# Cross-attention in two-step cycles of five TensorE runs, with four probability buffers

## What is computed

```python
def _L0_xattn_ref(hidden_states, audio_tokens, attention_mask, Wq, bq, Wk, bk, Wv, bv, Wo, bo, ...):
    q = proj(hs, Wq, bq, S); k = proj(at, Wk, bk, T); v = proj(at, Wv, bv, T)     # 16 heads of 16
    scores = jnp.einsum('bhsd,bhtd->bhst', q, k) / scale
    ...                                                     # clip, mask to -10000, clip to -50..50
    probs = jax.nn.softmax(scores, axis=-1)
    ctx = jnp.einsum('bhst,bhtd->bhsd', probs, v)
    delta = rs * (ctx @ Wo.T + bo)                          # then layernorm, added to x

x = x + _L0_attn_ref(_layernorm(x), ...)
x = x + _L0_xattn_ref(_layernorm(x), ctx_2048, mask_BxS2_ik0, ...)
x = x + _L0_ffn_ref(_layernorm(x), ...)                     # bit_linear(silu(gate) * val)
```

## Times and profile before

| | us |
|---|---|
| median of 3 timed runs | 1391.47 (1391.31 to 1391.74) |
| the profiled execution, its own time | 1393.63 |
| its span, first to last instruction | 1391.8 |
| TensorE busy in the span | 1369.9 |
| VectorE / ScalarE / GpSimd busy | 996.4 / 719.7 / 512.0 |
| mean granted TensorE clock | 0.998 of full speed |

### The profile page before, as it was taken

The page is one execution under the profiler, slowest core; times in us unless marked ns, Lnnn a source line. Parts: engine busy times, 40 slices in busy tenths (PEclk is TensorE's granted clock), DMA queues, the critical chain, the costliest instruction groups (busy, mean ns, idle before and its releaser), DMA issues.

```text
span 1391.8 us, 55872 instructions
## 1 busy us (share of the span) xinstructions
PE 1369.9 (98%) x25409; PEld 1171.4 (84%) x25409; DVE 996.4 (72%) x1824; ACT 719.7 (52%) x943; POOL 512.0 (37%) x491
## 2 busy tenths in 40 slices
PE   8999999999999999999999999999999999999997
PEld 6788888886888888888888888888888888888884
DVE  5688788785346867777676867677776868677766
ACT  3545454543555555555555555555554555555550
POOL 2656666551324233333323332433333242333310
PEclk9999999999999999999999999999999999999999
DMA  7010001010411211121212121121212112111100
GB/s 193 1 36 1 32 1 32 2 52 1 127 55 47 65 47 50 47 65 32 68 32 78 51 62 50 47 65 32 65 32 80 42 55 65 48 51 47 51 3 8
DMA packets 38957, 66.81 MB, mean 48 GB/s; under 512 B 3749, under 2 KB 36962, under 8 KB 38722
## 3 DMA queue, kind: packets, MB, share of 16 engines
q1 hardware_dynamic: 38722, 63.24, 15.6%
HBM read 61.40 MB, written 1.84 MB: 45 GB/s over the span
## 4 chain that ended last, share of the span: by engine, by line
PE 72%; DVE 2%; issue 0%; POOL 0%; DVEq 0%
PE proj_ps L1479 20%; PE proj_ps L1470 20%; PE score_ps L1497 15%; PE sum_ps L1522 13%; PE side_ps L1557 2%; PE side_ps L1571 1%; PE side_ps L1539 1%; PE side_ps L1564 1%; DVE amax L1357 0%; DVE hidden L1379 0%; DVE sig L1389 0%; DVE hidden L1390 0%; PE side_ps L1546 0%; DVE exps L1279 0%; DVE totals L1301 0%
## 5 line engine op out<-in xcount | busy, mean ns | idle before, releaser
L1231 ACT ACTIVATE exps<-score_ps 125x1792 f32<-125x1792 f32 x192 | 320.4, 1669 | 431.0 <-PE score_ps L1497 431.0
L1279 DVE TENSOR_SCALAR exps<-exps,top 125x896 f32<-125x896 f32 x384 | 287.9, 791 | 21.8 <-ACT exps L1231 17.5
L1497 PE MATMUL score_ps<-spread,keys 32*125 32x112 f32 x6144 | 219.0, 279 | 0.0
L1270 DVE COPY vals<-proj_ps 125x512 f32<-125x512 f32 x192 | 129.5, 687 | 116.7 <-PE proj_ps L1479 114.4
L1522 PEld LDWEIGHTS sum_ps<-exps,vals 125*32 125x32 f32 x12288 | 163.1, 110 | 47.1 <-issue 34.2
L1497 PEld LDWEIGHTS score_ps<-spread,keys 32*125 32x125 f32 x6144 | 184.8, 183 | 15.4 <-issue 0.3
L1522 PE MATMUL sum_ps<-exps,vals 125*32 125x56 f32 x12288 | 191.6, 215 | 0.0
L1159 POOL TENSOR_TENSOR low<-raw_early,high 128x500 fp32r<-128x500 f32 x64 | 84.5, 1322 | 216.8 <-PE proj_ps L1470 215.9
L1159 POOL TENSOR_TENSOR low_early<-raw_early,high_early 128x500 fp32r<-128x500 f32 x62 | 89.4, 1459 | 168.7 <-PE proj_ps L1470 168.7
L1223 ACT ACTIVATE keys<-proj_ps,b_k 128x500 f32<-128x500 f32 x192 | 129.9, 677 | 23.9 <-PE proj_ps L1470 20.4
L331 POOL TENSOR_TENSOR swapped<-swapped,sin 128x448 f32<-128x448 f32 (+1 forms) x69 | 81.0, 1175 | 85.6 <-ACT swapped L615 80.3
(11 more groups left out here) (187 smaller groups left out, 2702.7 us busy)
## 6 DMA issues: line engine op xcount, KB each, us to landing
raw_early<-in_ctxT SPq DMA_DIRECT2D x64, 500.0 KB, 4.2
raw<-in_ctxT SPq DMA_DIRECT2D x32, 500.0 KB, 3.6
w_q<-in_attn_Wq SPq DMA_DIRECT2D x4, 512.0 KB, 9.6
out<-y_out SPq DMA_DIRECT2D x16, 112.0 KB, 2.5
rows<-in_x SPq DMA_DIRECT2D x1, 1344.0 KB, 18.1
raw_early<-in_attn_Wo SPq DMA_DIRECT2D x1, 1024.0 KB, 17.5
raw_early<-in_ffn_gate_wT SPq DMA_DIRECT2D x1, 1024.0 KB, 5.3
raw_early<-in_ffn_val_wT SPq DMA_DIRECT2D x1, 1024.0 KB, 4.9
```

The lines of the kernel that those rows point to most:

```text
L1231: nc.scalar.activation(exps[t % 2][:, :, :, :].rearrange("p h r n -> p r h n"), score_ps[0:TILE, :, 0:2 * QW].rearrange("p r (h n) -> p r ...
L1270: nc.vector.tensor_copy(vals[r][:, 2 * q:2 * q + 2, :, 0:HD], proj_ps[q][0:TILE, :].rearrange("p (k h d) -> p k h d", k=2, d=HD))\
L1279: nc.vector.tensor_scalar(tile, tile, LIMIT_LO, top[:, n, at:at + 1], ALU.max, ALU.min)\
L1497: ins = nc.tensor.matmul(score_ps[0:TILE, r, to:to + HE * S], keys[c % 2][32 * r:32 * r + 32, k, (at + half) * TILE:(at + half + 1) * TILE ...
```

## The change

It does four things in `block_b`.

1. The number of probability buffers `exps` goes from 2 to 4 (`SLOTS`), and the exponential of step `t` waits for the value product of step `t - 4` instead of `t - 2`.
2. TensorE goes over a chunk's two steps in one cycle: scores of the even step, pieces 0 and 1, scores of the odd step, the value products of both steps *of the cycle before*, pieces 2 and 3. The steps after attention keep their numbers: an even one comes behind the even scores, an odd one behind the value products.
3. ScalarE makes both exponentials of the cycle first, then the copies of the two keys pieces with the `split_high` between them.
4. VectorE clips the probabilities in their own step (no longer one late), and makes both values copies at the end of the cycle, behind the step after attention of the odd step. `read_sums` comes behind the clip of the even steps 0 and 6.

```diff
-GATES = (7, 8)
-AFTER = (2, 5)
+TWINS = NT // 2
+SLOTS = 4
...
-        exps = [sb(f"exps{n}", [TILE, 2, HR, QW]) for n in range(2)]
+        exps = [sb(f"exps{n}", [TILE, 2, HR, QW]) for n in range(SLOTS)]
...
-                    act.wait_ge(probs_used, NT * i + t - 1)
+                    act.wait_ge(probs_used, NT * i + t - SLOTS + 1)
...
# ScalarE
             def body(i, first, last):
-                for t in range(NT):
-                    c, half = divmod(t, 2)
-                    x = PC * i + c
-                    exp_twin(i, t, not first or t >= 2)
-                    if half == 0:
-                        for p in range(DC):
-                            if not (last and c == PC - 1):
-                                keys_out(x + 1, p, (c + 1) % 2)
-                            if not (last and c >= PC - 2):
-                                split_high((c + 2) % 3, 2 * i + (c + 2) // 3 + 1, c % 2, p)
-                    if not first and t in GATES:
-                        gate_tanh(i - 1, GATES.index(t))
+                for m in range(TWINS):
+                    x = PC * i + m
+                    exp_twin(i, 2 * m, not first or 2 * m >= SLOTS)
+                    if not first and m == 4:
+                        gate_tanh(i - 1, 1)
+                    exp_twin(i, 2 * m + 1, not first or 2 * m + 1 >= SLOTS)
+                    for p in range(DC):
+                        if not (last and m == PC - 1):
+                            keys_out(x + 1, p, (m + 1) % 2)
+                        if not (last and m >= PC - 2):
+                            split_high((m + 2) % 3, 2 * i + (m + 2) // 3 + 1, m % 2, p)
+                    if not first and m == 3:
+                        gate_tanh(i - 1, 0)
...
# VectorE
-                for t in range(NT):
-                    c, half = divmod(t, 2)
+                for m in range(TWINS):
+                    e, o = 2 * m, 2 * m + 1
+                    if e in AHEAD and e in tail:
+                        tail[e]()
                     for k in range(2):
-                        if t:
-                            limit(i, t - 1, k)
-                        elif not first:
-                            limit(i - 1, NT - 1, k)
-                    if t == 1 and not first:
+                        limit(i, e, k)
+                    if e == 0 and not first:
                         read_sums(i - 1, 1)
-                    if t == BN + 1:
+                    if e == BN:
                         read_sums(i, 0)
-                    if t in tail and t not in AFTER:
-                        tail[t]()
-                    if last and t == BN + 3:
+                    if e in tail and e not in AHEAD:
+                        tail[e]()
+                    for k in range(2):
+                        limit(i, o, k)
+                    if o in tail:
+                        tail[o]()
+                    if last and o == BN + 3:
                         divide(i, 0)
...
+                    for q in range(2) if not (last and m == PC - 1) else ():
+                        values_copy(PC * i + m + 1, q, (m + 1) % 2)
...
# TensorE
+                for m in range(TWINS):
+                    e, o = 2 * m, 2 * m + 1
+                    x, r = PC * i + m + 1, (m + 1) % 2
+                    scores(i, e, not first or e >= 1)
+                    if e in tail:
+                        tail[e]()
+                    if not (last and m == PC - 1):
+                        piece(x, 0, r)
+                        piece(x, 1, r)
+                    scores(i, o, True)
+                    for n in (e - 2, e - 1):
+                        if n >= 0:
+                            add_up(i, n, not first or n >= BN)
+                        elif not first:
+                            add_up(i - 1, NT + n, True)
+                    if o in tail:
+                        tail[o]()
+                    if not (last and m == PC - 1):
+                        piece(x, 2, r)
+                        piece(x, 3, r)
+                    else:
                         pe.wait_ge(vals_ready, 2 * PC * PAIRS)
                         spare(3)
-                    if t == NT - 1 and not first:
+                        add_up(i, e, True)
+                    if o == NT - 1 and not first:
                         tail[NT]()
```

30 lines of the change are left out of this document (4 added, 26 removed).

## The result

The changed kernel takes 1577.75 us (median of 4 runs, 1572.99 to 1585.45) against 1391.39 of the kernel before beside it: ratio 1.134, 95% interval 1.133 to 1.136. The forecast was 1509, with 1474 to 1542 as its range: the sign was right, the size was short by 69 us. The profiled execution took 1572.99 and its span is 1571.2, that is 179.4 more than before.

The account below looks back on a forecast made before the run. TensorE, busy 98% of the span, was taken to bound the kernel. New waits less saved boundaries add 102 us to 1391.5, giving 1494; ten clock falls add 15, giving 1509 us, range 1474 to 1542.

Parts of the forecast that it names:

- The boundary: TensorE: joining two value products leaves five boundaries a chunk instead of six; 0.11 us each, 0.66 saved per pair.
- The keys wait: TensorE before piece 2, every cycle: keys copy 0 comes behind the second exponential; 0.77 us, net 0.67, partly covered by side products.
- pair 0: First pair, no side work: six cycles each longer by 0.67 less 0.11, together 3.4 us; chunk near 10.5 against 9.92.
- The gate wait: TensorE, cycle 3: up(1) waits for gates(0), which now stands behind read_sums on VectorE; 2.3 us, 2.2 net.
- The values-copy wait: TensorE before piece 0 of cycle 2: values copy 0 stands behind add_delta; 2.87 us, net 2.76, or 2.3 if power takes 0.59.
- The price of a fall: TensorE's granted clock dropping to 1.2 GHz after a long wait: between 1.3 and 1.7 us lost, taken as 1.5.
- four buffers alone: ScalarE's exponential no longer waits for the value product two steps before: worth nothing alone, but makes the new order possible.
- The step that failed: VectorE's values copy 0 judged covered: 0.5 us to spare in cycle 0, 0.4 in cycle 4.
- one fall for three long waits: TensorE's clock: some 30 waits of 2.3 to 2.8 us, one in three followed by a fall; 10 falls, +15 us.
- rival B: TensorE's clock stays up through all waits: 1494 us; chance 0.26.
- Rival C: TensorE's clock falls behind every long wait, 30 x 1.5 = 45: 1539 us, above 1545 if short waits count; chance 0.17.
- The prediction's E: Keys copy 0 is there when value products end, long waits covered, 95 boundaries gained: faster, 1381 to 1372 us; chance 0.04.

Follow-up runs that it names:

- The cut split: Changed kernel with GpSimd's split_low cut from 500 to 20 columns from context chunk 3 on: 1502.87 us, ratio 1.080 to the kernel before.
- One of the last experiments: Changed kernel with three orders mended, values copies ahead of add_delta and silu(1), and split_low cut to 20 columns: 1403.70 us, ratio 1.010.

## Why the prediction was wrong in size

*What held.* The boundary: 0.64 a pair measured for 0.66, partly by luck, since a joined cycle without side work saves 0.14 for my 0.11 and cycle 1 is 0.10 longer for a reason that stays open. The keys wait: 0.64 with a hand-over of 0.05 (keys copy 0 begins at 888.12 and ends 0.67 later) instead of 0.77 with 0.10. It hides no boundary (cycle 0 is 10.49 with it and 9.78 without), where I had 0.11, so that the net came out as forecast is two small errors that cancel; pair 0's undisturbed cycles are 10.50, as forecast. In cycles 4 and 5 the wait is too short to be listed, so it is 41 times in the list, not 75 to 90, but the cycle is 0.20 longer for my 0.19. The gate wait, 2.33 for 2.3. The values-copy wait, 2.50 for 2.87: the power took 0.54, the case that the prediction priced at 2.3. The price of a fall, 1.5. That four buffers alone are worth nothing.

*The step that failed* is the sentence "Checked the same way and found covered: values copy 0 in cycle 0, behind `read_sums` and `divide`, has some 0.5 to spare; in cycle 4, behind `silu(1)`, 0.4". I walked VectorE's list there with the durations of an undisturbed VectorE, and asked only after the copy, not after `project`, which needs the divide. ScalarE's new order, by which I had moved `split_low` in cycle 1, moves it in every cycle, and in cycles 0 and 4 it lands on VectorE's clips and on `silu(1)`. Its 2.5 to 3.0 us then lengthen VectorE's chain. That cost (2.16 – 0.56) x 14 = 22 in cycle 1 and (1.08 – 0.18) x 14 = 13 in cycle 5. The cut split shows it: both terms go. What ScalarE's order has to do with it differs. With the old order the collision of cycle 0 is gone; that of cycle 4 only moves from `silu(1)` to `silu(0)`, and cycle 5 pays the same wait of 0.81.

The Trainium skill, "SBUF — State Buffer", section "Who interferes with whom", says that VectorE shares a pair of ports with GpSimd, that `copy`, `cast` and `tensor_scalar` can take both and instructions with two SBUF inputs need the shared one, and that the one that comes second blocks fully. The traces agree as to which instructions are hit: 3.19 for 1.28 (`tensor_scalar`), 1.22 for 0.27 and 1.63 for 0.69 (two inputs), 2.56 for 0.35, each beside a `split_low`. This rule bore on the change, and the prediction did not weigh it.

*The clock.* The prediction took one fall for three long waits, 10 in all. There were 22; 19 of the 30 long waits were followed by one. The count came from waits of 1.2 to 1.45, and the new ones have 2.3 and 2.5; I had written that against rival B and not drawn it into the number. Rival C, a fall behind each of the 30, was about as far off on the other side. The Trainium skill ("TensorE: Matmul & The Clock Gate", section "HAM oscillation") describes a kernel whose every pass leaves TensorE idle long enough and pays the half clock in every pass. The trace here does not show that: waits of 2.0 to 2.5 in every pass were followed by a fall in 19 of 30 cases.

*The gaps.* Twelve, 13.2 us, and the two in `turn_hidden`, 1.4 us, in no sentence of the prediction.

*Pair 0.* Its first cycle has no value products of a cycle before, which cover the keys elsewhere: the wait is 2.35, that is 0.64 and the missing 1.71, and the clock fell behind it. The cycle took 12.89 for 9.00; I had priced it like the others.

*The ledger.* The forecast for the profiled span was 117 us more (its terms add to 102.7 before the clock, where it writes 102); it was 179.4, so 62 are missing. The undisturbed cycles of pairs 1 to 14 give (9.28 – 6.70) x 14 = 36, nearly all of it cycles 1 and 5. Falls and gaps in these pairs are 33.7, where 15 stood for the whole kernel: 19 more. (19 falls of 1.5 are 28.5 and the gaps 13.2, of which a wait behind a gap absorbs some 8.) Pair 0 adds 5, the last pair 5 (two falls and its heads wait). The span before pair 0 was 2.3 shorter. Rounding apart, that is the 62.

*The order as such.* The prediction's E gave the joined products 1372 to 1381 if all waits were covered. One of the last experiments came nearest to that case: no wait on another engine in the pairs, no fall, and 1404. Why it is not below 1391 is the gaps, and what makes them is shown only so far: most are in value products of 128 instructions in a row, they nearly vanish when these stand apart, remain without context loads, keep their places as long as TensorE's list stays as it is, and follow a transfer of the instruction queue by 0.6 to 1.8 us. The excess of the mean over the undisturbed pair is 1.5 x 14 = 21 us. Of these, 16.8 are gaps with no releaser: 12.8 in joined value products, 2.4 in `turn_hidden` and 1.6 in the values pieces, both of which stand right behind them. Where the other 4 lie I did not find out.

No version that I ran beats the kernel before.

## What to carry to other kernels

When an order is changed, don't only ask when each result comes; lay VectorE's and GpSimd's new times over each other, and where a long GpSimd instruction falls on VectorE's, add its length to that chain. A term "found covered" by half a microsecond is not covered when a 2.5 us instruction of the neighbour has moved. The trace of the kernel before can show the danger, in collisions that cost nothing yet. And on an engine at 98%, an order that opens a wait can pay twice, once for the wait and once more for the clock, 1.5 us each behind 19 of the 30 waits of some 2 us and more here; repairing one wait of VectorE mostly moved it to the next, until its work was in another place.

## What the runs showed of the hardware

- TensorE seems to run short of instructions when many short ones stand in a row; no view shows the shortage itself. The joined value product is 128 matmuls in 1.71 us, and 10 to 14 gaps of up to 1.9 us came up in each version with joined products, at places that only a change of TensorE's own list moved. With 64 in a row there were three, of 0.9 at most, in one kernel and none in the kernel before, so the number in a row is not all of it. The instruction queue moved 3.29 MB in 201 transfers in the changed kernel as in the one before, so the amount is not what differs.
- A new kind of boundary is no dearer: scores to value product, and the rest of the new order, gave 0.14 a cycle where the keys pieces' edges gave 0.11 (9.78 against 9.92 in cycles without side work).
- What a VectorE instruction loses beside GpSimd had little to do with its own length: 0.27 became 1.22, 0.35 became 2.56, and two clips of 1.28 became 3.19. Not every one is hit: the product of `values_`, which reads `side_ps` and `val_b`, took 0.74 beside a `split_low` (L1380, at 1304.26) and 0.75 without (at 1299.83).
- Two waits of 2.0 to 2.5 us in each pair gave a clock fall in 19 of 30 cases, in the same program with the same work around it. Kernels that differ by one moved or held step had 17, 22, 26 and 31 falls in all, so a count taken from one kernel can be off by ten for its neighbour.
